# Three edits in a four-layer graph kernel: one more group of the gated layer is turned by VectorE and DMA, ScalarE rounds half of the states, ScalarE writes psi's bias

## The reference, cut to what matters

```python
x = _layernorm(x + attention(x, adj))
# layer 1: gated, 5 steps, in_matrix = out_matrix = adj
    u3 = h @ u3_w.T + u3_b
    z = sigmoid(av @ w3_w.T + w3_b + u3)          # av = [adj @ h, adj @ h]
    r = sigmoid(av @ w4_w.T + w4_b + u3)
    hv = tanh(av @ w5_w.T + w5_b + (r * h @ u5_w.T + u5_b))
    h = (1.0 - z) * h + z * hv
x = _layernorm(x + chebyshev_conv(x, adj))        # layer 2
# layer 3
    features = relu(x @ psi_w + psi_b)
    messages = (adj * adj).T @ features
    h = relu(concat(messages, x) @ phi1_w + phi1_b)
x = _layernorm(x + h @ phi2_w + phi2_b)
```

## Time and profile before

| | |
|---|---|
| median of 3 runs | 1312.88 us |
| profiled execution, its time | 1311.03 us |
| its span | 1309.2 us |
| TensorE busy | 1270.0 us, 97% |
| VectorE busy | 1066.5 us, 81% |
| GpSimd busy | 1019.4 us, 78% |
| ScalarE busy | 979.3 us, 75% |
| mean granted TensorE clock | 0.994 |

### The profile page before, as it was taken

One profiled execution on the slowest core, in us unless ns is written; L12 is line 12 of the kernel. 1 busy time (PEld: TensorE's weight loads), 2 busy tenths in 40 slices (PEclk: granted clock), 3 DMA queues, 4 the chain that ended last, 5 costly groups with the idle time before them and its releaser, 6 DMA issues.

```text
span 1309.2 us, 27304 instructions
## 1 busy us (share of the span) xinstructions
PE 1270.0 (97%) x8126; PEld 1134.5 (87%) x8126; DVE 1066.5 (81%) x2522; ACT 979.3 (75%) x1767; POOL 1019.4 (78%) x1019
## 2 busy tenths in 40 slices
PE   8999989999999999999999999998799999999997
PEld 7999977888888888888888888886589999999996
DVE  4788877888888888888888888888688888888886
ACT  4788878778788787887877888877456777777774
POOL 5988888888888888888888888888456666666654
PEclk9999999999999999999999999999999999999999
DMA  3233332533323533324334223342033222222211
GB/s 111 82 98 108 102 114 71 150 86 81 97 56 83 151 81 88 82 62 140 93 88 98 59 71 87 88 128 82 19 96 89 73 71 70 71 68 74 71 33 41
DMA packets 143005, 111.71 MB, mean 85 GB/s; under 512 B 13906, under 2 KB 114132, under 8 KB 142932
## 3 DMA queue, kind: packets, MB, share of 16 engines
q1 hardware_dynamic: 142500, 110.68, 31.5%
q10 hardware_dynamic: 432, 0.20, 0.1%
HBM read 60.49 MB, written 50.33 MB: 85 GB/s over the span
## 4 chain that ended last, share of the span: by engine, by line
PE 86%; DVE 4%; POOL 4%; issue 3%; ACT 2%; DMA 1%; SPq 0%; POOLq 0%; ACTq 0%; DVEq 0%
PE psum L1296 6%; PE psum L855 5%; PE psum L857 5%; PE psum L383 4%; PE psum L1308 3%; PE psum L1310 3%; PE psum L898 3%; PE psum L899 3%; PE psum L900 3%; PE psum L875 3%; PE psum L870 3%; PE psum L887 3%; PE psum L874 3%; PE psum L869 3%; PE psum L888 3%
## 5 line engine op out<-in xcount | busy, mean ns | idle before, releaser
L790 POOL TENSOR_TENSOR rh_lo<-rh,rh_hi 128x512 fp32r<-128x512 f32 x160 | 207.5, 1297 | 40.2 <-ACT rh_hi L949 40.0
L797 POOL TENSOR_TENSOR h_lo<-h,h_hi 128x512 fp32r<-128x512 f32 x160 | 209.5, 1309 | 11.5 <-ACT h_hi L922 1.7
L970 DVE TENSOR_TENSOR psum<-psum,h 128x512 f32<-128x512 f32 x160 | 111.9, 699 | 103.5 <-ACT psum L953 103.5
L855 PE MATMUL psum<-adj_t_hi,hn_hi 128*128 128x256 f32 x640 | 161.4, 287 | 4.0 <-DVE m_lo L986 4.0
L936 ACT ACTIVATE psum<-psum,bias_cols 128x512 f32<-128x512 f32 x160 | 106.2, 664 | 76.6 <-PE psum L875 74.7
L857 PE MATMUL psum<-adj_t_hi,hn_lo 128*128 128x256 f32 x640 | 156.8, 280 | 0.0
L804 POOL TENSOR_TENSOR hn_lo<-hn,hn_hi 128x512 fp32r<-128x512 f32 x96 | 124.0, 1292 | 37.4 <-ACT hn_hi L944 37.4
L949 ACT CAST rh_hi<-rh 128x512 fp32r<-128x512 f32 x160 | 99.6, 623 | 71.1 <-DVE rh L992 71.1
L855 PEld LDWEIGHTS psum<-adj_t_hi,hn_hi 128*128 128x128 f32 x640 | 120.9, 189 | 9.6 <-issue 5.1
L857 PEld LDWEIGHTS psum<-adj_t_hi,hn_lo 128*128 128x128 f32 x640 | 120.6, 188 | 4.4
L986 DVE TENSOR_TENSOR m_lo<-psum,m_hi 128x512 fp32r<-128x512 f32 x160 | 108.7, 679 | 10.9 <-ACT m_hi L931 10.9
(11 more groups left out here) (277 smaller groups left out, 4323.9 us busy)
## 6 DMA issues: line engine op xcount, KB each, us to landing
h_dram<-squares SPq DMA_DIRECT2D x512, 64.0 KB, 1.8
hn<-h_dram SPq DMA_DIRECT2D x96, 256.0 KB, 2.7
x_in<-in_x_dram SPq DMA_DIRECT2D x32, 256.0 KB, 3.0
x_dram<-x SPq DMA_DIRECT2D x32, 256.0 KB, 2.1
g_x<-x_dram SPq DMA_DIRECT2D x32, 256.0 KB, 4.7
ht<-h_dram SPq DMA_DIRECT2D x32, 256.0 KB, 2.8
c_x<-x_dram SPq DMA_DIRECT2D x32, 256.0 KB, 3.0
out_dram<-res SPq DMA_DIRECT2D x32, 256.0 KB, 2.4
```

The source lines that it names most:

```text
L790: pool.tensor_tensor(rh_lo[:, q, :], rh[:, q, :], rh_hi[:, q, :].bitcast(F32), ALU.subtract).then_inc(rh_lo_done, 1)
L797: pool.tensor_tensor(h_lo[:, q, :], h[:, (g - 1) % G, :], h_hi[:, q, :].bitcast(F32), ALU.subtract).then_inc(h_lo_done, 1)
L855: pe.matmul(dst, hn_hi[:, p, tile(b, c), :], adj_hi[:, c, :], start=(b == 0 and c == 0), stop=False, skip_group_check=True)
L970: dve.tensor_tensor(cb, cb, hg, ALU.subtract).then_inc(dif_done, 1)
```

## The change

`MOVED` becomes all groups but 0. In steps 2 to 5 of a set group 4 is no longer turned by TensorE: it goes through VectorE's squares, five DMAs, ScalarE's rounding from SBUF and GpSimd's subtraction, as the other six do. In the first step its matmul inputs still come from x1, now rounded one slot ahead. The two buffers of hn and of squares are taken by g % 2, and semaphore counts are recomputed (`step`, `counted`, `prior`). Which engine rounds h is now decided by `hi_kind`, g % 2: ScalarE for groups 0, 2, 4, 6, GpSimd for 1, 3, 5, 7. In the last layer psi's bias is loaded once, broadcast to 128 partitions (`psi_b`); for each group ScalarE copies it over four tiles into bank B_F, right behind the copy of x3t, and the psi matmuls accumulate on that. The bias matmul L1334 is gone from the 30 slots of the loop; the last two groups, in `drain`, keep theirs.

```diff
-    MOVED = [1, 2, 3, 5, 6, 7]
+    MOVED = [1, 2, 3, 4, 5, 6, 7]
...
     def kind(g):
-        return 1 if g % 4 else 0
+        return 1 if g % G else 0
...
+    def hi_kind(g):
+
+        return g % 2
...
+    def prior(g):
+
+        return g - 2 if g > 2 else G - g
...
     def place(g):
-        return MOVED.index(g) % 2
+        return g % 2
...
             if live(base, g, 1):
                 q = (g - 1) % 2
-                if kind(g - 1):
-                    pool.tensor_copy(h_hi[:, q, :], h[:, (g - 1) % G, :]).then_inc(h_hi_done[1], step(g - 1))
-                pool.wait_ge(h_hi_done[kind(g - 1)], counted(base, g - 1))
+                if hi_kind(g - 1):
+                    pool.tensor_copy(h_hi[:, q, :], h[:, (g - 1) % G, :]).then_inc(h_hi_done[1], 2)
+                pool.wait_ge(h_hi_done[hi_kind(g - 1)], hi_counted(base, g - 1))
...
-            if live(base, g, 1) and not kind(g - 1):
+            if live(base, g, 1) and not hi_kind(g - 1):
                 if first(at):
                     act.wait_ge(h_copied, k * G + g)
                 wait_count(act, r_mm, s - 2)
-                act.copy(h_hi[:, 0, :], h[:, g - 1, :]).then_inc(h_hi_done[0], 4)
+                act.copy(h_hi[:, 0, :], h[:, g - 1, :]).then_inc(h_hi_done[0], 2)
...
                 pe.wait_ge(x3t_done, m + 1)
-                wait_count(pe, hid_done, m)
-                if isinstance(it, int) and m == 0:
-                    pe.wait_ge(earlier["h_done"], GATED)
-                pe.matmul(psum[:, B_F, :], ones[:, :], flat(psi_row[:, :, :]), start=True, stop=False,
-                          skip_group_check=True)
+                pe.wait_ge(bias_set, m + 1)
                 for i in range(TILES):
...
                 act.copy(x3t[:, :], psum[:, B_T23, :]).then_inc(x3t_done, 1)
+
+                if isinstance(it, int) and m == 0:
+                    act.wait_ge(earlier["h_done"], GATED)
+                wait_count(act, hid_done, m)
+                act.copy(psum[:, B_F, :].rearrange("p (i d) -> p i d", d=D),
+                         env["psi_b"][:, :].rearrange("p (o d) -> p o d", o=1).broadcast_to([128, TILES, D]))\
+                   .then_inc(bias_set, 1)
```

More of the change, by code:

```diff
@@ L82, in adj_resnorm_d4_kernel @@
         phi2_b = keep("phi2_b", [128, D])
+        psi_b = keep("psi_b", [128, D])
         env = dict(locals())
@@ L264, in slot @@
                   .then_inc(rest_loaded, 16)
+                sp.dma_start(env["psi_b"][:, :], t["L3_gnn_psi_b"].rearrange("(o d) -> o d", o=1).broadcast_to([128, D]))\
+                  .then_inc(rest_loaded, 16)
                 sp.dma_start(phi1x[:, :], t["L3_gnn_phi1_w"][D:2 * D, :]).then_inc(phi1m_loaded, 16)
@@ L268, in sync @@
         yield from run(sp, slot, LAG_STORE)
-        sp.wait_ge(rest_loaded, 16 * 4)
+        sp.wait_ge(rest_loaded, 16 * 5)
         for q in range(2):
@@ L638, in gated_layer @@
     h_lo_done, rh_hi_done, rh_lo_done = (sem(n) for n in ("h_lo_done", "rh_hi_done", "rh_lo_done"))
-    h_hi_done = [sem("h_hi_done_turned"), sem("h_hi_done_moved")]
+    h_hi_done = [sem("h_hi_done_even"), sem("h_hi_done_odd")]
     rh_done, dif_done, inc_done, h_done = (sem(n) for n in ("rh_done", "dif_done", "inc_done", "h_done"))
@@ L690, in kind, with hi_counted @@
     def kind(g):
-        return 1 if g % 4 else 0
+        return 1 if g % G else 0
     def step(g):
-        return (4, 1, 1, 2)[g % 4]
+        return (G, 1, 1, 1, 1, 1, 1, 2)[g]
     def counted(base, g):
-        return base + g // 4 * 4 + (4, 1, 2, 4)[g % 4]
+        return base + (0 if g < 0 else G if g in (0, G - 1) else g)
+    def hi_kind(g):
+        return g % 2
+    def hi_counted(base, g):
+        return base + g // 2 * 2 + 2
+    def prior(g):
+        return g - 2 if g > 2 else G - g
     def squared(k, at, g):
@@ L739, in move @@
             store(k, at, g, place(g))
-            n, base = MOVED.index(g), k * SET_SLOTS + at
-            if n > 1:
-                sp.wait_ge(hn_lo_done[1], counted(base + G, MOVED[n - 2]))
+            base = k * SET_SLOTS + at
+            if g > 2:
+                sp.wait_ge(hn_lo_done[1], counted(base + G, prior(g)))
             elif at > 0:
-                sp.wait_ge(hn_lo_done[1], counted(base, MOVED[n - 2]))
+                sp.wait_ge(hn_lo_done[1], counted(base, prior(g)))
             sp.wait_ge(h_out[g], stored(k, at, g))
@@ L941, in slot @@
                 else:
-                    act.wait_ge(hn_loaded[place(g + 1)], k * 192 + at * 6 + (16 * (MOVED.index(g + 1) // 2 + 1) - 48))
+                    each = (3, 4)[place(g + 1)]
+                    act.wait_ge(hn_loaded[place(g + 1)], k * (64 * each) + at * (2 * each) + 16 * (g // 2 + 1 - each))
                 wait_count(act, m_mm, s)
@@ L978, in slot @@
                                   hn_hi[:, 0, :, :].rearrange("p i d -> p (i d)").bitcast(F32),
-                                  ALU.subtract).then_inc(hn_lo_done[0], 4)
+                                  ALU.subtract).then_inc(hn_lo_done[0], G)
             if live(base, g, 4):
@@ L1005, in squares_of @@
             if at == final:
-                held = (k, final, left - 2) if left > 1 else (k, final - G, MOVED[left - 2])
+                held = (k, final, left - 2) if left > 1 else (k, final - G, left + G - 2)
                 turn_squares(k, at, left, left % 2, held)
             elif kind(left):
-                n = MOVED.index(left)
-                held = (k, at, MOVED[n - 2]) if n > 1 else (k, at - G, MOVED[n - 2]) if at > 0 else \
-                    (k - 1, final, MOVED[n - 2]) if k > 0 else None
+                held = (k, at, prior(left)) if left > 2 else (k, at - G, prior(left)) if at > 0 else \
+                    (k - 1, final, prior(left)) if k > 0 else None
                 turn_squares(k, at, left, place(left), held)
@@ L1031, in gated_layer @@
     sems = {"h_out": h_out, "hn_lo_done": hn_lo_done[0], "m_lo_done": m_lo_done, "z_done": z_done,
-            "rh_done": rh_done, "h_done": h_done, "slots": SLOTS, "h_stored": tuple(stored(0, SET_SLOTS - G, g) for g in range(4)), "pairs_end": SLOTS - G}
+            "rh_done": rh_done, "h_done": h_done, "slots": SLOTS, "h_stored": tuple(stored(0, SET_SLOTS - G, g) for g in range(G)), "pairs_end": SLOTS - G}
     return programs, (earlier, sems)
@@ L1098, in graph_conv_layers @@
     y1_loaded = [sem(f"y1_loaded{i}") for i in range(2)]
-    y1_done = sem("c_y1_done")
+    y1_done, bias_set = sem("c_y1_done"), sem("c_bias_set")
     res_out = [sem(f"res_out{i}") for i in range(2)]
@@ L1177, in load @@
             if isinstance(it, int) and s < 8:
-                sp.wait_ge(earlier["h_out"][s], earlier["h_stored"][s % 4])
+                sp.wait_ge(earlier["h_out"][s], earlier["h_stored"][s])
             if isinstance(it, int) and s == 8:
                 for g, done in enumerate(earlier["h_out"]):
-                    sp.wait_ge(done, earlier["h_stored"][g % 4] * GROUPS // 8)
+                    sp.wait_ge(done, earlier["h_stored"][g] * GROUPS // 8)
             sp.dma_start(ht[:, u % 2, :], h_dram[bass.ds(s, 1), :, :].rearrange("o p c -> (o p) c"))\
```

## The result

The changed kernel takes 1302.82 us (median of 4 runs, 1300.74 to 1304.34) against 1312.54 for the kernel before; the ratio is 0.9922, 95% interval 0.991 to 0.9934. The difference of the medians is 9.7 us and the ratio makes it 10.2 (8.7 to 11.8 by its interval), where 9.85 was forecast. Runs of one kernel differ by up to 3.6 us here, with TensorE's mean granted clock: the two runs at 0.994 took 1300.74 and 1301.35, the two at 0.991 and 0.992 took 1304.3.

What follows compares the result with a forecast made beforehand. TensorE, busy throughout, was taken as the bound. Turns 6.75, less seam 0.3, plus psi's bias 3.4 gave 9.85 us off the 1312.88 median: 1303.0 us, own spread 1301 to 1305, wider range 1298.5 to 1309.0.

Steps and rivals of the forecast that it cites:

- TensorE sets the pace, so what is taken from it comes off: Gated and last layers: TensorE has no idle time, so removed time is gained until another engines' chain ends later.
- the 6.75 of the sum: Gated layer: 15 removed turns of h at 0.45 us each, one of the 16 being covered by a wait.
- The other engines hide what they took over: Gated layer: added work on VectorE, ScalarE, GpSimd and SyncE costs 0 us in the steady part.
- 0.17 us to spare and 0.05 of delay: Gated layer, chain to rh_lo: 0.17 us spare before TensorE's load, 0.05 us delay expected from squares, so no loss.
- the forecast of no wait for rh_lo in the steady part: Gated layer: slots of 4.37 us seven times of eight, with no TensorE wait on rh_lo.
- rival 3: Gated slots 1, 3 and 7: the chain over hn_lo and rh_lo runs late, 20.6 us lost, 1323.6 us; chance 0.08.
- The seam, -0.3: End of the gated layer, where TensorE waits for others: added VectorE or GpSimd work costs 0.3 us, 0.7 at most.
- Psi: 0.13 of 0.23 us: Last layers: of a bias matmul's 0.23 us, 0.13 is gained per slot, the rest waits for c_lo; 3.4 us over 26 slots.
- 0 to 0.03 per slot: Last layers: cost of psi waiting 0.09 to 0.15 us for the bias copy, mostly inside the 0.12 lost to c_lo.
- The copy itself: Last layers: ScalarE's copy of psi's bias from SBUF into PSUM takes 0.61 us, or 0.59 by the skill's rule.
- Rival 1: Both parts: all of TensorE's removed time comes off, 7.2 + 6.9 = 14.1 us, 1298.8 us; chance 0.14.
- Rival 2: Last layers: psi waits for a late or longer bias copy, so the bias gives nothing; 1306.4 us; chance 0.20.

Runs made afterwards that it cites:

- experiment 9: Changed kernel without psi's bias in the loop's 30 slots, plus one 512-column matmul per last-layer slot ahead of the wait for c_lo: 1301.28 us, one run.
- experiment 1: Changed kernel with psi's bias matmul put back in place of ScalarE's copy, so only the gated layer's edits remain: 1305.12 us, ratio 0.9949.
- experiment 3: Changed kernel with h rounded as before, ScalarE for groups 0 and 4, GpSimd for the other six: 1302.68 us, ratio 0.993.
- experiment 4: Kernel before with only the rounding of h moved, ScalarE for even groups and GpSimd for odd: 1313.66 us, ratio 1.0008.
- experiment 2: Kernel before with only the psi bias edit, ScalarE's copy replacing the bias matmul: 1308.96 us, ratio 0.9975.
- experiment 5: Changed kernel plus one 512-column matmul per last-layer slot, just ahead of the first adj matmuls, where TensorE waits for c_lo: 1308.1 us, ratio 0.9964.
- experiment 6: Changed kernel plus one 512-column matmul per last-layer slot, behind the first eight adj matmuls: 1308.47 us, ratio 0.9966.
- experiment 8: Changed kernel with two weight matmuls moved ahead of psi and the second power's adj matmuls taking all hi parts first: 1298.16 us, ratio 0.9891.
- experiment 10: Changed kernel without psi's bias in the loop's 30 slots, plus one 512-column matmul per last-layer slot behind the first eight adj matmuls: 1307.99 us, one run.
- experiment 7: Changed kernel without psi's bias in the loop's 30 slots, neither ScalarE's copy nor a matmul: 1302.75 us, ratio 0.9917.

## Why the prediction was right, step by step

- **TensorE sets the pace, so what is taken from it comes off.** Right in the gated layer. A turn was priced at 0.45. Over 15 turns the nine traces with this code give 0.39 (the changed kernel) to 0.46 (experiment 9), 0.43 on average: 5.9 to 7.0 us, on average 6.4, for the 6.75 of the sum. 0.45 is near the upper end.
- **The other engines hide what they took over.** Right, to a few tenths of a microsecond in all: experiments 1, 3 and 4. The chain over hn_lo and rh_lo was given 0.17 us to spare and 0.05 of delay. It was tighter than that in some slots, above all in those around the end of a set's first step, and the forecast of no wait for rh_lo in the steady part was wrong in that. There GpSimd makes hn_lo behind ScalarE's rounding of hn, then rh_lo, and the load of TensorE waits (the changed kernel):

```profile
596.96 1.29 POOL L818 TENSOR_TENSOR hn_lo<-hn,hn_hi 128x512 fp32r<-128x512 f32 x1
...
598.21 1.30 POOL L804 TENSOR_TENSOR rh_lo<-rh,rh_hi 128x512 fp32r<-128x512 f32 x1
...
599.57 0.19 PEld L901 LDWEIGHTS psum<-rh_hi,ug_hi 128*128 128x128 f32 x1 [0.18 <-POOL rh_lo L804]
599.66 0.41 PE L901 MATMUL psum<-rh_hi,ug_hi 128*128 128x512 f32 x1
```

rh_lo ends at 599.51, the load follows 0.06 later, 0.09 ahead of its matmul. That slot took 4.40 us instead of 4.37. So rival 3 is wrong in size, not in kind.
- **The seam, -0.3.** Not settled, and no loss shows. From slot 150 to the first psi matmul the clock is 0.96 in the kernel before and in experiments 1, 2, 5, 6, 8 and 10. The two with the old gated code need 81.6 and 81.5 us there, the five with the new one 80.3 to 81.9; a few tenths cannot be told.
- **Psi: 0.13 of 0.23 us.** The step was right that c_lo would take back part of it, and named the place; that c_lo itself does not move is right too (in the regular slots of every trace it ends 3.05 to 3.06 us behind the slot's first conv matmul). Measured are 0.10 a slot, 2.5 to 2.8 us over the psi distance and not 3.4. The copy is not what is missing. Its hand-over to psi took 0.11, where I took the 0.06 of c_lo and f_lo, but experiment 7 has the same regular slot without it, so it costs 0, the lower end of the "0 to 0.03 per slot". What is mis-sized is the 0.13 itself, 0.11 at c_lo and 0.02 behind it. The load for c_lo did come 0.12 earlier, yet it now stands 0.07 ahead of its matmul instead of 0.12, and the message matmuls come only 0.10 earlier.
- **The copy itself**, taken at 0.61, is 0.596. The nearest ScalarE pass from SBUF to SBUF takes 0.614 in the same trace (L936, which also rounds, so the two differ in more than where they write). That agrees with the sentence cited in the prediction from the Trainium skill (ScalarE: Activation LUTs, "Step-by-step: what each stage is for"), that ScalarE is faster into PSUM than into SBUF.
- **Rival 1** (14.1 us) fails at c_lo; experiment 8, which gives c_lo more cover, gets the slot down to the 10.67 that it would have meant. **Rival 2** (nothing from the bias) fails by experiment 2. Its worry was half right: psi waits for the copy in every slot, but the 0.06 that this costs is covered by c_lo.

That 1302.82 meets 1303.0 so closely is partly luck: the two main terms were 10.15 together and the traces show about 9.1 for them (6.4 and 2.7), 0.3 was taken off for a seam that shows none, and the medians scatter by more than the difference.

## What to carry to other kernels

When the busiest engine has no idle time, price a removed instruction by the distance of starts, then look how far behind it the next chain is: the time between a producer's end and the consumer's weight load, less the hand-over, 0.05 to 0.11 us here. If two such chains follow each other, their gaps do not add: the first to be late uses up cover of the second, and removing one wait shows the next. And where cover is short, moving work of the busy engine ahead of the wait, with what doesn't depend on the late half going first, took another 3.3 us off this stretch with no instruction removed.

## What the runs showed of the hardware that I had not expected

- The hand-over to TensorE's weight load was 0.05 to 0.06 us behind results of VectorE and GpSimd, and also behind ScalarE's activation of r into PSUM (it ends at 903.49 in the changed kernel, L912's load comes at 903.54). Behind ScalarE's copy of the bias it was 0.11 in every regular slot (1109.79 to 1109.90). So the engine that made the result doesn't decide it; what does is open.
- A load that is late costs far less than its lateness behind matmuls of 512 columns, where it usually stands 0.23 ahead of its own. In experiments 1 and 3 the matmuls before and after such a load are 0.46 us apart, 0.46 to 0.48 when it stands 0.10 to 0.17 ahead, and about 0.49 on average when it stands 0.06 to 0.09 ahead. So the 17 more late loads of experiment 3 come to about half a microsecond.
- In the gated layer some slots without a turn take 4.40 to 4.43 and not 4.37 us, with starts of matmuls 0.24 instead of 0.23 apart here and there, at a granted clock of 1.00. Of the 142 slots there were 24 such before (one is 587.52 to 591.91) and 17 to 37 in the nine traces with the new code: 36 in the changed kernel, which gained 0.39 a turn, and 17 in experiment 9, which gained 0.46. What causes them is open.
